# Edge pass of a graph attention layer: sums over heads, one-hots and weighted values for four steps per VectorE instruction instead of two

## The reference

```python
scores = jnp.einsum('ehd,ehd->eh', q[dst], k[src]) * scale
m = jax.ops.segment_max(scores, dst, num_segments=n)
ex = jnp.exp(scores - m[dst])
z = jax.ops.segment_sum(ex, dst, num_segments=n)
attn = ex / z[dst]
agg = jax.ops.segment_sum(attn[:, :, None] * v[src], dst, num_segments=n)
```

## Time and profile before

| | |
|---|---|
| median of 3 runs | 5206.49 us (5199.6 to 5270.99) |
| profiled execution | 5177.41 us, its span 5175.5 us |
| mean granted TensorE clock | 0.907 of full speed |
| TensorE, VectorE busy | 3953.5 us (76%), 3264.5 us (63%) |
| ScalarE, GpSimd busy | 1793.7 us (35%), 1943.6 us (38%) |
| VectorE instructions | 7493 |
| first edge pass | about 436 to 1878 us |
| second edge pass | about 2640 to 4120 us |

### The profile page before, as it was taken

How to read it: one execution, slowest core, us unless ns; L and a number is a source line. 1 busy time by engine, 2 the same in 40 slices (tenths; PEclk the granted TensorE clock), 3 DMA queues, 4 the chain that set the end, 5 groups by cost and what they waited for, 6 DMA issues and landing times. The chain is left out here.

```text
span 5175.5 us, 84744 instructions
## 1 busy us (share of the span) xinstructions
PE 3953.5 (76%) x17828; PEld 2700.2 (52%) x17829; DVE 3264.5 (63%) x7493; ACT 1793.7 (35%) x4909; POOL 1943.6 (38%) x1887
## 2 busy tenths in 40 slices
PE   2775778877878756999967777777778649999994
PEld 1443444444444434777734444444444328888883
DVE  4775777777777754555547776777777654444444
ACT  0112444444444421222224444444444403333331
POOL 2115666666666611000046665565566300000000
PEclk8997899898998877999989998998899869999997
DMA  3225666666656611111146666565566310000001
GB/s 73 87 86 169 174 182 182 179 181 172 187 171 187 173 46 52 57 57 54 53 142 185 179 174 172 170 178 169 168 179 177 113 51 26 24 24 24 24 17 50
DMA packets 347567, 617.38 MB, mean 119 GB/s; under 512 B 106280, under 2 KB 198506, under 8 KB 347338
## 3 DMA queue, kind: packets, MB, share of 16 engines
q0 software_dynamic: 136960, 447.68, 29.7%
q1 hardware_dynamic: 210538, 168.89, 11.4%
HBM read 563.57 MB, written 53.61 MB: 119 GB/s over the span
## 5 line engine op out<-in xcount | busy, mean ns | idle before, releaser
L669 POOL DMA_INDIRECT edge_kv<-kv,edge_idx x1664 | 1794.9, 1079 | 1118.9 <-issue 430.8
L848 PE MATMUL edge_sums<-edge_kv,edge_sel 128*128 128x272 f32 x3328 | 1057.9, 444 | 595.2 <-ACT edge_sums L916 363.3
L848 PEld LDWEIGHTS edge_sums<-edge_kv,edge_sel 128*128 128x128 f32 x3328 | 622.2, 206 | 890.3 <-issue 792.3
L915 ACT COPY acc<-edge_sums x1664 | 643.0, 386 | 1271.3 <-PE edge_sums L848 491.6
L801 PE MATMUL edge_q<-qc,edge_spread 128*128 x3328 | 965.5, 416 | 126.3 <-issue 61.1
L801 PEld LDWEIGHTS edge_q<-qc,edge_spread 128*128 128x128 f32 x3328 | 634.4, 205 | 367.4 <-issue 285.0
L916 ACT COPY edge_sums<-edge_blank 128x272 f32 x1664 | 658.5, 396 | 3.2 <-issue 3.2
L711 DVE TENSOR_TENSOR edge_kv<-edge_kv,edge_q 128x512 f32<-128x512 f32 x832 | 558.4, 671 | 103.4 <-PE edge_q L801 56.9
L760 DVE TENSOR_TENSOR edge_kv<-edge_kv 128x512 f32<-128x512 f32 x832 | 566.8, 681 | 7.9 <-ACT edge_kv L905 7.2
L718 DVE TENSOR_REDUCE edge_score<-edge_kv 128x16 f32<-128x512 f32 x832 | 561.3, 675 | 0.2
L733 DVE TENSOR_TENSOR_SCAN edge_up<-edge_flags,edge_turned 64x128 f32<-64x128 f32 x208 | 85.7, 412 | 443.4 <-PE edge_turned L830 277.4
(11 more groups left out here) (352 smaller groups left out, 4744.2 us busy)
## 6 DMA issues: line engine op xcount, KB each, us to landing
edge_rel<-step_rel SPq DMA_DIRECT2D x208, 256.0 KB
edge_kv<-kv,edge_idx POOLq DMA_INDIRECT x1664
edge_flags<-step_flags SPq DMA_DIRECT2D x416, 32.0 KB
kv<-first_kv_out SPq DMA_DIRECT2D x25, 512.0 KB
kv<-middle_kv_out SPq DMA_DIRECT2D x25, 512.0 KB
end_rows<-edge_ends SPq DMA_DIRECT2D x416, 8.5 KB
h<-first_h SPq DMA_DIRECT2D x25, 256.0 KB
middle_h_in<-h SPq DMA_DIRECT2D x25, 256.0 KB
```

Source lines behind the costliest of these rows:

```text
L669: nc.gpsimd.indirect_dma_start(kv[:, turn[0], j, 0:KV], None, dram["kv"], bass.IndirectOffsetOnAxis(ap=idx[:, turn[0], j:j + 1], axis=0)). ...
L848: pe_p.tick(t.matmul(psa[:, bass.ds(place[j % 2], QC)], sel[:, j, :], kv[:, turn[0], j, D:ROW], start=False, stop=True, skip_group_check=T ...
L915: s.copy(acc[:, bass.ds(at, QC)], psa[:, bass.ds(bank, QC)])
```

## The change

The sums over heads are made once for steps 0 to 3, at the place of `("score", 1)`, and once for steps 4 to 7, at the place of `("score", 3)`; at the places of scores 0 and 2 nothing is done. One-hots and weighted values are made for steps 4 to 7 at the place of `("late", 2)` and for steps 0 to 3 at the place of `("tail", 0)`; at `("late", 3)` and `("tail", 1)` VectorE does nothing. The products stay as they are, two steps each, and so do all instructions of TensorE, ScalarE, GpSimd and SyncE; only the counts for which they wait are other ones: the matmuls of the first two steps of a half now wait for the value of all four. The one-hots wait until TensorE has used those of all four steps of the half before them.

```diff
--- before.py
+++ after.py
@@ -529,11 +529,11 @@
         act_p = Progress(nc, ctx, f"edge{layer}_act", 4)
         pe_p = Progress(nc, ctx, f"edge{layer}_pe", 4)
         dve_steps = ["spread"]
-        for m in range(PAIRS):
-            dve_steps += [f"product{m}", f"score{m}"]
+        for half in range(2):
+            dve_steps += [f"product{2 * half}", f"product{2 * half + 1}", f"score{half}"]
         dve_steps += ["up", "top", "below", "maxima"]
-        for m in range(PAIRS):
-            dve_steps += [f"sel{m}", f"value{m}"]
+        for half in range(2):
+            dve_steps += [f"sel{half}", f"value{half}"]
         dve_p.begin(dve_steps)
         pe_p.begin([f"q{m}" for m in range(PAIRS)] + ["score_t", "max_t"] 
                    + [f"sums{j}" for j in range(HALF)] + ["ends0"] + [f"sums{j}" for j in range(HALF, G)] + ["ends1"])
@@ -594,7 +594,7 @@
             def load_rest(turn, wait=True):
                 if wait:
                     before = later(turn, -4)
-                    dve_p.wait(sp, before, f"value{PAIRS - 1}", beside=s_clear)
+                    dve_p.wait(sp, before, "value1", beside=s_clear)
                     act_p.wait(sp, before, "ends1", beside=s_clear)
                 slot = turn[0]
                 s = s_table[slot]
@@ -713,11 +713,13 @@
                         if m == 0 and not end:
                             spread_of(later(turn, 1), begun == 0)
                     elif what == "score":
-                        k_rows = kv[:, turn[0], 2 * m:2 * m + 2, 0:D]
-                        dve_p.wait(dve, turn, f"product{m}")
-                        dve_p.tick(v.tensor_reduce(
-                            score[:, lane, 2 * m * H:2 * (m + 1) * H].rearrange("p (j h) -> p j h", h=H),
-                            k_rows.rearrange("p j (h d) -> p j h d", h=H), AX.X, ALU.add), turn, f"score{m}")
+                        if m % 2 == 1:
+                            first = (m - 1) * 2
+                            k_rows = kv[:, turn[0], first:first + HALF, 0:D]
+                            dve_p.wait(dve, turn, f"product{m}")
+                            dve_p.tick(v.tensor_reduce(
+                                score[:, lane, first * H:(first + HALF) * H].rearrange("p (j h) -> p j h", h=H),
+                                k_rows.rearrange("p j (h d) -> p j h d", h=H), AX.X, ALU.add), turn, f"score{m // 2}")
                     elif what == "up":
                         if owner is not None:
                             scan_up(owner)
@@ -746,20 +748,20 @@
                     dve_p.tick(v.tensor_tensor(kv[:, turn[0], :, KV + H:ROW], psm.rearrange("p (j h) -> p j h", h=H),
                                                bc(tab[:, turn[0], :, 1:2], [P, G, H]), ALU.mult),
                                turn, "maxima")
-                elif what in ("tail", "late"):
+                elif what in ("tail", "late") and m % 2 == 0:
+                    half, at = m // 2, 2 * m
 
                     if not earliest:
-                        pe_p.wait(dve, later(turn, -1), f"sums{2 * m + 1}")
-                    at = 2 * m
-                    dve_p.tick(v.tensor_tensor(sel[:, at:at + 2, :], bc(keep["cols"][:, :].unsqueeze(1), [P, 2, P]),
-                                               bc(tab[:, turn[0], 2 * m:2 * m + 2, 0:1], [P, 2, P]),
-                                               ALU.is_equal), turn, f"sel{m}")
-                    if m == 0:
+                        pe_p.wait(dve, later(turn, -1), f"sums{at + HALF - 1}")
+                    dve_p.tick(v.tensor_tensor(sel[:, at:at + HALF, :], bc(keep["cols"][:, :].unsqueeze(1), [P, HALF, P]),
+                                               bc(tab[:, turn[0], at:at + HALF, 0:1], [P, HALF, P]),
+                                               ALU.is_equal), turn, f"sel{half}")
+                    if half == 0:
                         act_p.wait(dve, turn, "weights")
-                    values = kv[:, turn[0], 2 * m:2 * m + 2, D:KV].rearrange("p j (h d) -> p j h d", h=H)
+                    values = kv[:, turn[0], at:at + HALF, D:KV].rearrange("p j (h d) -> p j h d", h=H)
                     dve_p.tick(v.tensor_tensor(values, values,
-                                               bc(kv[:, turn[0], 2 * m:2 * m + 2, KV:KV + H].unsqueeze(3), [P, 2, H, DH]),
-                                               ALU.mult), turn, f"value{m}")
+                                               bc(kv[:, turn[0], at:at + HALF, KV:KV + H].unsqueeze(3),
+                                                  [P, HALF, H, DH]), ALU.mult), turn, f"value{half}")
 
             spread_of((0, None, 0), True)
             groups_of(dve, body)
@@ -826,7 +828,7 @@
                     elif what == "product":
                         ahead_of(turn, m, places, begun)
                     elif what == "turn":
-                        dve_p.wait(pe, turn, f"score{PAIRS - 1}", beside=s_clear)
+                        dve_p.wait(pe, turn, "score1", beside=s_clear)
                         pe_p.tick(t.transpose(pst, score[:, turn[0] % 2, :], keep["ident"][:, :]), turn, "score_t")
                     elif owner_of(what, turn, begun) is not None:
                         rest(owner_of(what, turn, begun), what, m, places, is_first(owner_of(what, turn, begun)))
@@ -838,7 +840,7 @@
                     pe_p.tick(t.transpose(psm, top[:, :], keep["ident"][0:G * H, 0:G * H]), turn, "max_t")
                 elif what in ("tail", "late"):
                     place = places[m] if m in places else sums_at(turn, m)
-                    dve_p.wait(pe, turn, f"value{m}")
+                    dve_p.wait(pe, turn, f"value{m // 2}")
 
                     if m > 0:
                         act_p.wait(pe, turn, f"acc{2 * m - 1}")
```

## The result

The changed kernel takes 5441.62 us (median of 4 runs, 5433.68 to 5462.0), the kernel before beside it 5204.69 (5199.6 to 5270.99): ratio 1.0428, 95% interval 1.0365 to 1.049. Forecast were 5214 us, range 5119 to 5305. The profiled execution has a span of 5431.8 us against 5175.5.

The account below looks back on a forecast made before the run. VectorE was taken to wait for TensorE in the edge passes, so its net 0.13 us saved per turn was worth 0; late first halves (5 us) and pass ends (3 us) added 8: 5214 us, no change, range 5119 to 5305.

Parts of the forecast that it names:

- VectorE's busy time: Whole kernel: 1248 VectorE instructions fewer; busy time down 60 to 90 us, idle time up by about as much.
- The second score behind its product: VectorE's second sum over heads waits for the product just ahead: 0.29 us added per turn, bounds 0 and 0.29.
- The idle time before the sums over heads: VectorE's idle time was to rise by some 0.2 us before each second sum over heads.
- the wait of the scatter matmuls on the merged value: TensorE's scatter matmuls waiting for a weighted value: idle time up from 21.5 us, still under 80.
- The short wait before L747: VectorE's subtraction (before: L745) starts 0.25 us sooner, with a new 0.14 us wait for TensorE's transpose.
- The late first half: Values of steps 0 to 3 reach TensorE 0.04 us late per full-clock turn: at most 8 us, 5 taken.
- Rival D: GpSimd's gather issues held up by longer VectorE runs: 5435 us at 0.5 longer per issue, likelier under 20 us; chance 0.06.
- the fast turns still 10.3 to 10.5: Edge passes: sign of a right forecast, the fast turns keep their length of 10.3 to 10.5 us.
- the clock at 0.90: Edge passes: sign of a right forecast, TensorE's granted clock stays at 0.90 as before.
- what would make it fail altogether: Edge passes: slow turns, their long stops unexplained by the trace, coming more or less often with VectorE's new rhythm.
- Rival C: TensorE idles in one piece for late first-half values, clock granted less often: 5308 us, or 5410; chance 0.14.
- a clock of 0.87 or less: Edge passes: sign that the forecast is wrong and the rival of TensorE's lower granted clock holds.

Follow-up runs that it names:

- e13: Changed kernel with the gathers of the odd steps left out, four per turn in place of eight, their tiles constant: 4511.05 us, ratio 0.866.
- e1: Kernel before with only the sums over heads merged, one-hots and weighted values still made for two steps each: 5192.71 us, ratio 0.9932.
- e3: Changed kernel with the weighted values back in two instructions per half at their old four places; one-hots and sums stay merged: 5216.61 us, ratio 1.0012.
- e4: Kernel with only the one-hots merged, sums over heads and weighted values made for two steps each: 5263.3 us, ratio 1.0073 to the kernel before.
- e5: Changed kernel, but of the weighted values only those of steps 0 to 3 merged, those of 4 to 7 in two at old places: 5213.34 us, ratio 1.0053.
- e6: Changed kernel, but of the weighted values only those of steps 4 to 7 merged, those of 0 to 3 in two at old places: 5289.19 us, ratio 1.0174.
- e2: Changed kernel with the sums over heads made for two steps each again; one-hots and weighted values stay merged: 5428.69 us, ratio 1.0384.
- e7: Changed kernel with each merged value written as two instructions, one directly behind the other at the merged one's place: 5411.18 us, ratio 1.0422.
- e8: Changed kernel with each merged value as two adjacent instructions, TensorE waiting for both before a half's first two steps: 5415.52 us, ratio 1.0437.

## Why the place costs: what holds TensorE's results back

**e9_after_paced, e10_before_paced: gathers spread over the turn**, the changed kernel and the one before.

```diff
-                    if not first:
+                    if not first and j in (0, 1, 4, 5):
                         pe_p.wait(pool, later(turn, -LANES), f"ends{j // HALF}", beside=s_clear)
+                    elif not first:
+                        dve_p.wait(pool, later(turn, -2), {2: "product0", 3: "product1", 6: "product2", 7: "product3"}[j],
+                                   beside=s_clear)
```

> The changed kernel, but GpSimd spreads the eight gathers of a turn over the turn: gathers 0, 1, 4 and 5 wait for the ends of the turn four places before, as now, and 2, 3, 6 and 7 for the four products of the turn two places before. Theory H (TensorE's signals reach the other engines only in lulls of the gather traffic, and the new order falls into a cycle with eight gathers issued in a row every second turn): the long stops before the subtraction of the maxima go, the loss goes, 5100 to 5230. Rival R (the new order costs by its dependences alone, whatever the gathers do): 5400 to 5450, with the same stops. Rival P (later gathers make VectorE wait for rows): above 5450, with idle time before the products.

> The kernel before with the same spread gathers. Theory H: it gains too, if less, 5050 to 5170, with fewer turns over 15 us. Rival R: 5180 to 5220, no change. Rival P: above 5250.

Measured: e9 5462.23 us, ratio 1.0443 (1.0401 to 1.0484); e10 5214.73, ratio 0.9978 (0.9955 to 1.0002). By the numbers that is rival R, but the test decides nothing: what GpSimd waited for in e9 shows that the added waits were nearly always fulfilled already, so that the gathers were hardly spread.

```profile
POOL edge_kv L672 <- PE edge_end_sums L864: 789.7, 170, 11.6
...
POOL edge_kv L672 <- DVE edge_kv L714: 2.4, 8, 0.3
```

**e11_after_half_rows, e12_before_half_rows: half of the bytes per gather** (the value elements are left out of the gathers and constant).

```diff
-                        kv[:, turn[0], j, 0:KV], None, dram["kv"],
+                        kv[:, turn[0], j, 0:D], None, dram["kv"],
...
```

> The changed kernel with gathers that bring only the 256 key elements of a row, half of the bytes; the value elements keep a constant written once at the start of each pass (some 20 us more in all), so the weighted sums are of other data. The instructions of all engines are the same. Theory H: the stops shrink with the traffic, turns of 10.5 to 12 us, 4650 to 4950 in all. Rival R: above 5350.

> The kernel before with the same half rows (the value elements are left out of the gathers here too). Theory H: 4650 to 4950 and within 1% of e11_after_half_rows, since the difference between the two orders is only in how they meet the traffic. Rival R: some 4% faster than e11_after_half_rows.

Measured: e11 5444.33 us, ratio 1.0401 (1.036 to 1.0443); e12 5230.51, ratio 0.9994 (0.9964 to 1.0025). Neither kernel gains anything from half of the gathers' bytes (VectorE is busy 14.5 us longer in e11, for the constants, so a gain of a few tenths of a per cent could hide); theory H, as far as it laid the stops to bytes, falls.

**e13_after_half_gathers, e14_before_half_gathers: half of the gather instructions** (the gathers of odd steps are left out, their tiles constant, and with them the waits of VectorE and SyncE for those rows; all work of the other engines stays). Half of the rows and of their landings go with the instructions, where e11 kept them all.

```diff
-                for j in range(G):
+                for j in range(0, G, 2):
...
```

> The changed kernel with the gathers of the odd steps left out: four per turn in place of eight, each with its whole rows, the other four tiles keep a constant written once per pass (so half of the edges are other data). Bytes as in e11_after_half_rows, but half of the gather instructions and of the row descriptors. Theory G (it is GpSimd's issuing of gathers, not their bytes, that keeps TensorE's signals and SyncE's instructions back): the stops before the subtraction vanish, turns of 10.5 to 11.5 us, 4600 to 4850 in all. Rival D (the stops are made by the dependences among TensorE, VectorE and ScalarE alone): 5350 to 5450, no change.

> The kernel before with the same four gathers per turn. Theory G: 4600 to 4850, and within 1.5% of e13_after_half_gathers, since what the new order costs is only how it meets the gathers. Rival D: 5150 to 5250.

Measured: e13 4511.05 us, ratio 0.866 (0.8602 to 0.8717); e14 4497.09, ratio 0.8632 (0.8574 to 0.8689). The stops are gone, and so is the difference between the two orders: 0.3% where it was 4.3%. The kernel before gains 13.7% by it and the changed one 17%, so the gathers held up the old order as well, if less. What the changed order waits for in e13:

```profile
POOL edge_kv L669 <- PE edge_end_sums L862: 1276.6, 400, 11.7
...
DVE edge_below L748 <- PE edge_turned L841: 147.7, 198, 1.6
...
DVE edge_below L748 <- remote: 8.0, 2, 4.3
```

and its first pass by stretch, then the bytes of the gather queue (packets, MB, share) in e11 and in e13:

```profile
421.70:1534.60 1112.90, 1004.00 (x5123) 611.27 (x5122) 1020.09 (x1543) 648.03 (x1947) 382.00 (x403) 1.00 0.45 129
```

```profile
q0 software_dynamic: 83712, 229.57, 14.4%
```

```profile
q0 software_dynamic: 70400, 229.52, 17.1%
```

The unnamed waits fell from 1195.9 to 8.0 us and the clock of the pass rose from 0.88 to 1.00. e11 and e13 move the same bytes, 229.5 MB; with eight gather instructions per turn the kernel takes 5444 us, with four 4511. So it is the number of gathers and not their bytes; whether it is GpSimd's instructions, the rows (128 to a gather) or the signals of their landing, e13 can't tell apart. With four per turn GpSimd issues them in twos:

```profile
1104.56 0.95 POOL L669 DMA_INDIRECT edge_kv<-kv,edge_idx  x1 [3.11 <-PE edge_end_sums L862]
1105.81 0.94 POOL L669 DMA_INDIRECT edge_kv<-kv,edge_idx  x1 [0.30 <-issue]
...
1110.61 0.95 POOL L669 DMA_INDIRECT edge_kv<-kv,edge_idx  x1 [3.85 <-PE edge_end_sums L862]
```

**e15_after_two_in_flight, e17_after_three_in_flight, e18_before_three_in_flight: whole kernels in which GpSimd starts a gather only when the second (e15) or third before it has landed.** The wait in e17 and e18 (in e15 with 2 in place of 3):

```diff
+                    if j >= 3:
+                        wait_beside(pool, s_clear, *fill([s_row[i][j - 3] for i in range(LANES)], LANES, turn))
+                    elif not first:
+                        wait_beside(pool, s_clear, *fill([s_row[i][j + G - 3] for i in range(LANES)], LANES, later(turn, -1)))
```

> The changed kernel, whole, but GpSimd starts a gather only when the last but one before it has landed. Theory G in the form that a backlog of gathers does it (series of eight issued 1.25 us apart while each takes some 2 to 3 us to land): 5100 to 5300, the stops of over 4 us rarer than 30. If each issue does it, backlog or not: 5380 to 5480. If landing is so slow that gathers become the bound: above 5500, with idle time before the products.

> The changed kernel, whole, with at most three gathers on their way (a gather starts when the third before it has landed). Two in flight took 18.2 us per turn, 2.3 us per gather, so one landed some 4.5 us after its start; three would allow 1.5 us per gather, 12.2 us per turn, less than the 15.1 of the changed kernel. Theory G with a backlog of more than three as the source of the stops: 12.2 to 13 us per turn, 4850 to 5000 in all, stops of over 4 us rarer than 20. If three in a row are enough to hold TensorE's signals: 5250 to 5450. If landing takes longer with three on their way, so that gathers bound the turn: above 5450.

> The kernel before, whole, with at most three gathers on their way, as e17_after_three_in_flight. If the limit takes away what the new order loses and nothing else, the old order gains little from it: 5130 to 5200, within 1% of e17_after_three_in_flight (5180). If the limit helps every order alike: 4950 to 5050. If it only helps the long series of gathers that the new order makes, and its extra waits on GpSimd cost the old one: 5210 to 5300.

Measured: e15 6057.25 us, ratio 1.1628 (1.1551 to 1.1706); e17 5180.06, ratio 0.9889 (0.9848 to 0.993); e18 5188.71, ratio 0.9861 (0.9799 to 0.9923). In e15 no unnamed wait is left at all; the gathers bound the turn instead:

```profile
POOL edge_kv L673 <- DMA edge_kv<-kv,edge_idx: 1604.8, 861, 4.0
DVE edge_kv L715 <- DMA edge_kv<-kv,edge_idx: 1451.5, 824, 4.5
```

With three in flight both orders take the same time within their intervals. The changed order gets back all that it lost (ratio 1.0428 to 0.9889), the old one gains 1.4%. Both intervals lie below 1, but the gain is under 2%, and the kernel before itself had medians of 5191 and 5255 us in two sets of runs on one chip. What the old order gains by is not shown: its unnamed waits rise from 682 to 742 us. The 12.2 us per turn that I had hoped for did not come: the stops are rarer in e17 (273.6 us in 60 times before `below`, where the changed kernel has 449.4 in 87), not gone, although series of eight or more gathers without a pause (under 0.45 us between them) have all but gone, 2 where the changed kernel has 93.

**e16_after_two_stores: SyncE stores the ends of two turns with two transfers, not four.**

```diff
-                for q in range(HALF):
+                for w in range(2):
...
-                                 ends[32 * q:32 * q + 2, lane // 2, :, :]).then_inc(s_ends[lane // 2], 16)
+                                 ends[w:P:32, lane // 2, :, :]).then_inc(s_ends[lane // 2], 16)
```

> The changed kernel, whole, but SyncE stores the border sums of two turns with two transfers in place of four (one per row of a pair, over the four partition groups). These stores stand every second turn, as the long stops do. Theory S (the stops come from SyncE's issues of the stores): at least a third of the loss goes, 5250 to 5360. Theories G and D: 5390 to 5460, no change.

Measured: 5501.01 us, ratio 1.0558 (1.0483 to 1.0632), no gain; the 1% above the changed kernel is not clear of the two intervals. This theory S, that SyncE's stores make the stops, falls.

All runs, by the unnamed waits of the profiled execution (formed as above):

| kernel | us | ratio | unnamed waits, us |
|---|---|---|---|
| e15 two in flight | 6057 | 1.163 | 0 |
| e14, e13 half the gathers | 4497, 4511 | 0.863, 0.866 | 8, 8 |
| e1 scores merged | 5193 | 0.993 | 554 |
| before; e10 | 5205; 5215 | 1; 0.998 | 682; 692 |
| e3 values at old places | 5217 | 1.001 | 731 |
| e17, e18 three in flight | 5180, 5189 | 0.989, 0.986 | 742, 742 |
| e12 before, half rows | 5231 | 0.999 | 768 |
| e4; e5; e6 | 5263; 5213; 5289 | 1.007; 1.005; 1.017 | 867; 879; 919 |
| after; e11 half rows | 5442; 5444 | 1.043; 1.040 | 1196; 1228 |
| e2, e7, e8, e9 | 5429, 5411, 5416, 5462 | 1.038 to 1.044 | 1289 to 1319 |
| e16 two stores | 5501 | 1.056 | 1400 |

But for e15, which has another bound, times and unnamed waits rise roughly together; e17 and e18 lie 1% below the kernel before with more of such waits, so the index orders only differences larger than that.

## Why the prediction was wrong

**Right, or right but for a size.** 6245 instructions. Merged sums and values 1.14 us from start to start (1267.10 to 1268.24, 1268.95 to 1270.09; predicted 1.13), one-hots 0.60 (1266.50 to 1267.10). VectorE's busy time fell by 53 us, where 60 to 90 were predicted. The second score behind its product costs 0.71 from start to start (1268.24 to 1268.95), against 0.59 to a one-hot: 0.12 where I took 0.29 from the earlier trace rows. The Trainium skill, "VectorE: DVE Perf Modes", section "The DRAIN you can't avoid", says of a chain of copies that the semaphores between them cost nothing; the row shows 0.12, so the trace does not quite agree, but it is closer to the page than I was. The idle time before the sums over heads is 7.3 us in all, where 0.2 before each second one (42 us) was foretold; the wait of the scatter matmuls on the merged value fell to 5.1 us, where it was to rise from 21.5. The short wait before L747 is there: ready at 1264.33 + 1.14 = 1265.47, started at 1265.63. The late first half costs 0.09 us in the short turn (5.37 against 5.28), predicted 0.04. By these sizes the change would have cost some 20 us at most (208 x 0.09); e7 shows that merging as such costs nothing, e1 that the sums over heads even gain 0.7%. Rival D falls as I put it: the mean of GpSimd's issues went down, 1079 to 1037 ns. GpSimd's gathers had their part all the same (e13), but not through the length of the issues.

**Wrong: "the fast turns still 10.3 to 10.5"** and the clock at 0.90. The short turn shown takes 11.6 us, since the transpose reaches the scan 1.20 us late, turns under 11 us fell from 51 to 13, and the passes have 0.88 and 0.87. The step that failed is the sum's reach: it put the change in the slow turns at nothing. It went step by step along the dependences of one undisturbed turn, at full clock, and took the stops of the other turns as given; the time went into those stops. The text named this as what would make it fail altogether and gave it no chance or price, although showed 4.9 us in the neighbouring turn that were not VectorE's work: a third of that turn was outside the sum. Turns of over 18 us went from 18 to 72.

**Rival C had the size, not the cause.** It priced one turn of ten going from 10.43 to 15.32 at 102 us, and two at 204; measured are 237. But it laid this to TensorE idling for want of values and the clock falling. TensorE waits 5.1 us for values, and with half of the gathers the same order runs at a clock of 1.00. Its sign, a clock of 0.87 or less, was met in one pass and missed by 0.01 in the other, with another cause. In the stop shown above the lower clock comes behind the stop. The stretches from the transpose to TensorE's next matmul, and from there on:

```profile
1309.53:1315.66 6.13, 0.00 (x1) 0.01 (x1) 1.55 (x4) 1.49 (x5) 1.90 (x2) 0.67 0.54 164
1315.66:1319.00 3.34, 3.34 (x13) 1.50 (x14) 3.04 (x3) 1.49 (x6) 0.00 (x0) 0.50 0.39 80
```

TensorE stands still for 6.13 us, with the clock at 1.00 (2.4 GHz) in the 6.5 us before; behind that it has 0.50 (1.2 GHz), and four scatter matmuls take 2.17 us instead of 1.18. How much of the 237 us is the clock is not separated.

**What the runs showed in its place.** The values' place in VectorE's order decides (e3 against e7); it acts only together with GpSimd's gathers, eight to a turn and with no limit on their way (e13 against e14, e17 against e18); and not by bytes (e11). GpSimd's timeline around the long stop shown above:

```profile
1301.80 1.14 POOL L669 DMA_INDIRECT edge_kv<-kv,edge_idx  x1 [1.27 <-remote]
1303.24 1.00 POOL L669 DMA_INDIRECT edge_kv<-kv,edge_idx  x1 [0.30 <-issue]
...
1319.66 0.95 POOL L669 DMA_INDIRECT edge_kv<-kv,edge_idx  x1 [7.90 <-PE edge_end_sums L861]
```

From 1301.80 to 1310.81 it issues eight gathers without a pause, then waits 7.90 us for `ends`. The end of such a series and the end of the stop lie close together: of the 86 subtractions of the changed kernel that start over 2 us after the recorded end of their transpose (35 before), the middle half start 1.9 to 2.3 us after GpSimd's last issue has ended (here 1311.76 to 1314.08). But the series alone are not the difference: the kernel before has as many of eight or more (89 against 93). That such series and stops feed each other (the series holds TensorE's results back, the late `ends` make GpSimd pause, and after the pause it has places of two turns to fill) is my reading of it, and only argued. Open are why the earlier place of the values leads into this alternation, why the two halves are more than the sum of their parts, and what in the chip ties the gathers to late results of TensorE and slow moves of SyncE.

## What to carry to other kernels

Where slow turns stand beside fast ones and the profile cannot name what ended their waits, find that cause before costing an edit on the fast turn: a sum over dependences says nothing on how often the slow ones come. A change of place on one engine can then cost 4% without any instruction or dependence that costs it; e7 and e8 are the pattern to tell merging from moving. If GpSimd issues gathers in long series beside a busy TensorE, try a limit on how many are on their way: here three took away the whole loss of 4.3%, and two cost 16%. Fewer and larger gathers may be worth a trial; no run here made them.

## What the runs showed of the hardware

- While gathers follow one another, VectorE and ScalarE can go on with a result of TensorE 1.2, 4.6 and 7.1 us after its recorded end (1273.52, 1309.53, 1306.85), both within 0.3 us of each other in the stop shown; SyncE is slowed too (its four stores take 5.20 us from 1304.69 on, and 1.58 in a turn of e13):

```profile
1102.16 1.58 SPq L616 DMA_DIRECT2D end_rows<-edge_ends  x4
```

- It hangs on the number of gathers: with half of them the changed kernel falls from 5442 to 4511 us, with half of their bytes not at all (5444). With two on their way there is no such stop (e15), with three there still are some (e17).
- A gather of 128 rows of 2 KB, with one other on its way, landed 3.8 us after its start in the median of e15 (3.3 to 4.5). The Trainium skill, "DMA: Bandwidth & Descriptors", section "Anatomy of one DMA — SWDGE (gpsimd) path", gives 2.0 us plus bytes/436e3, an estimate of 2.6 us for 262 KB; the trace is 1.2 us above it:

```profile
DMA to landing us min/median/max: 3.3/3.8/4.5
```
